# Sixteen heads in six transfers: expanding queries and keys in whole rows instead of halves

## What is computed

```python
y = layernorm(x) * ln_w + ln_b
q, k, v = y @ wq, y @ wk, y @ wv              # per head: 256 x 8, 16 heads
weights = softmax(q @ k.T / sqrt(8) + causal) # 256 x 256 for each batch and head
x1 = layernorm(x + (concat(weights @ v) @ wo + x))
W_all = W + up_aux @ lora_up @ lora_down @ down_aux
out = layernorm(x1 + (x1 @ W_all.T + b))
```

## Time and profile before

| | |
|---|---|
| median of 3 runs | 601.8 us (598.26 to 603.31) |
| the profiled execution | 601.86 us |
| its span, first to last instruction | 599.8 us |
| PE busy | 471.4 us (79%) |
| DVE busy | 356.9 us (60%) |
| ACT busy | 293.9 us (49%) |
| POOL busy | 223.9 us (37%) |
| mean granted clock of PE | 0.836 of 2.4 GHz |
| DMA packets | 91422, of 70.26 MB |

### The profile page before, as it was taken

The page is one execution under the profiler, slowest core; times in us unless marked ns, Lnnn a source line. Parts: engine busy times, 40 slices in busy tenths (PEclk is TensorE's granted clock), DMA queues, the critical chain, the costliest instruction groups (busy, mean ns, idle before and its releaser), DMA issues. The chain is left out here.

```text
span 599.8 us, 26116 instructions
## 1 busy us (share of the span) xinstructions
PE 471.4 (79%) x10929; PEld 381.9 (64%) x10929; DVE 356.9 (60%) x1021; ACT 293.9 (49%) x615; POOL 223.9 (37%) x361
## 2 busy tenths in 40 slices
PE   6897876889888777797766898877785987896793
PEld 3465665677767665676665686666674766774572
DVE  5376555667565656575644765466566656674543
ACT  2625454555455445365543654455544554562470
POOL 6643232442344343243432523334424333422144
PEclk9758888888687799797978977689978878896897
DMA  2544444444444344444434444443444444434210
GB/s 72 153 126 120 125 124 110 115 130 127 126 126 137 112 118 123 130 125 129 136 95 129 126 131 118 127 133 108 129 123 129 126 127 124 128 105 115 74 49 27
DMA packets 91422, 70.26 MB, mean 117 GB/s; under 512 B 14428, under 2 KB 72627, under 8 KB 91315
## 3 DMA queue, kind: packets, MB, share of 16 engines
q1 hardware_dynamic: 89766, 67.69, 39.5%
q10 hardware_dynamic: 1548, 0.95, 0.6%
HBM read 47.07 MB, written 21.00 MB: 113 GB/s over the span
## 5 line engine op out<-in xcount | busy, mean ns | idle before, releaser
L943 DVE TENSOR_REDUCE rowmax<-max_bank 128x2 f32<-128x512 f32 (+3 forms) x352 | 220.4, 639 | 179.8 <-PE max_bank L1249 177.7
L596 ACT ACTIVATE probs<-score_bank 128x512 f32<-128x512 f32 x320 | 182.0, 598 | 139.1 <-PE score_bank L1267 76.0
L1245 PE MATMUL max_bank<-kx,qx 74*64 74x192 bf16 (+2 forms) x1536 | 130.0, 246 | 60.5 <-DMA kx<-k_rows 59.7
L1267 PE MATMUL score_bank<-qx,kx 106*64 106x64 bf16 x2048 | 140.5, 210 | 33.8 <-DMA qx<-mT 33.8
L1245 PEld LDWEIGHTS max_bank<-kx,qx 74*64 74x64 bf16 x1536 | 87.6, 126 | 76.9 <-DMA kx<-k_rows 63.5
L1267 PEld LDWEIGHTS score_bank<-qx,kx 106*64 106x64 bf16 x2048 | 106.9, 123 | 45.8 <-DMA qx<-mT 39.2
L1249 PE MATMUL max_bank<-kx,qx 106*64 106x64 bf16 x2048 | 130.1, 209 | 0.0
L1272 PE MATMUL score_bank<-qx,kx 74*64 74x192 bf16 (+2 forms) x1536 | 122.5, 240 | 0.0
L1289 PE MATMUL pv_bank<-probs,v_ext 128*32 128x256 f32 (+3 forms) x2048 | 97.1, 337 | 13.5 <-issue 13.5
L1249 PEld LDWEIGHTS max_bank<-kx,qx 106*64 106x64 bf16 x2048 | 98.0, 123 | 3.2 <-issue 0.4
L1289 PEld LDWEIGHTS pv_bank<-probs,v_ext 128*32 128x32 f32 x2048 | 63.6, 121 | 46.1 <-issue 29.6
(11 more groups left out here) (99 smaller groups left out, 586.0 us busy)
## 6 DMA issues: line engine op xcount, KB each, us to landing
kx<-k_rows SPq DMA_DIRECT2D x187, 96.0 KB
qx<-q_rows SPq DMA_DIRECT2D x128, 96.0 KB
qx<-q_rows SPq DMA_DIRECT2D x64, 104.0 KB
q_rows<-parts SPq DMA_DIRECT2D x32, 192.0 KB, 2.3
k_rows<-parts SPq DMA_DIRECT2D x31, 192.0 KB, 2.5
xa<-in_x SPq DMA_DIRECT2D x32, 128.0 KB, 2.4
xr<-in_x SPq DMA_DIRECT2D x32, 128.0 KB, 2.3
out<-y SPq DMA_DIRECT2D x32, 128.0 KB, 2.0
```

What stands on the lines that cost most here:

```text
L596: act.activation(probs[:, unit, :], score_bank[SCORE_BANK[unit]][:, :], ACT.Exp, scale=SCALE)\
L943: dve.tensor_reduce(to, b[:, 0:n * width].rearrange("p (w s) -> p w s", s=width), AX.X, ALU.max)\
L1245: pe.matmul(b[which * BLOCK:(which + 1) * BLOCK, at:at + width - BLOCK], q[0:SCORE_ROWS, h, s], k[0:SCORE_ROWS, h, 0:width - BLOCK], start ...
L1267: ins = pe.matmul(b[which * BLOCK:(which + 1) * BLOCK, at:at + BLOCK], k[0:DIAGONAL_ROWS, h, t], q[0:DIAGONAL_ROWS, h, t], start=True, sto ...
```

## The change

`expand` issues six transfers for a batch: three of queries and three of keys, each with all sixteen heads of its 24 (or 26) partitions, so a row is one piece of 8 KB. One semaphore `s_expand` counts them; `max_scores` waits for it at unit 0 alone. The same is done to the transfers of the first batch, two of which ACT issues (five before). In SP's step `load_xa(it, 4)` goes ahead of `store_parts`, and `load_xr` goes behind `expand` and is of the batch `it - 2`. The loads of xa and xr and the expansion have waits and `alone` increments in the loop that stood only in the written-out part. The order of the calls in `first`, `step` and `last` of every engine is a new one, with the same instructions in it; in the loop, PE has two waits fewer (`values`, `x_transpose`) and two more (`pv_transpose` of half 1, `feed_forward`).

```diff
 def load_xa(it, o):
-    if it.static:
-        sp.wait_ge(s_xhat, it.done(o - RING))
-    sp.wait_ge(s_xa, it.done(o - 1, 16))
+    used, landed = it.done(o - RING), it.done(o - 1, 16)
+    sp.wait_ge(s_xhat, used)
+    alone(sp, "sp")
+    sp.wait_ge(s_xa, landed)
...
 def expand(it, o):
...
-    for half in range(HALVES):
-        if half == 0:
-            sp.wait_ge(s_q_stored, it.done(o, 16))
-        else:
-            sp.wait_ge(s_expand[1], it.done(o - 1, EXPAND))
-        for turn in range(PARTS):
-            a, n = turn * PART_ROWS, PART_ROWS + (MAX_PARTS if turn == PARTS - 1 else 0)
-            sp.dma_start(of_half(qx[r][a:a + n, :, :], half), of_half(q[0:n, :, :], half)).then_inc(s_expand[half], 16)
-        if half == 0:
-            sp.wait_ge(s_stored, it.done(o, STORES))
-        for turn in range(PARTS):
-            a = turn * PART_ROWS
-            sp.dma_start(of_half(kx[r][a:a + PART_ROWS, :, :], half),
-                         of_half(k[turn * HD:turn * HD + PART_ROWS, :, :], half)).then_inc(s_expand[half], 16)
+    sp.wait_ge(s_expand, landed)
+    alone(sp, "sp")
+    sp.wait_ge(s_q_stored, q_stored)
+    for turn in range(PARTS):
+        a, n = turn * PART_ROWS, PART_ROWS + (MAX_PARTS if turn == PARTS - 1 else 0)
+        sp.dma_start(qx[r][a:a + n, :, :], q[0:n, :, :]).then_inc(s_expand, 16)
+    sp.wait_ge(s_stored, k_stored)
+    for turn in range(PARTS):
+        a = turn * PART_ROWS
+        sp.dma_start(kx[r][a:a + PART_ROWS, :, :], k[turn * HD:turn * HD + PART_ROWS, :, :]).then_inc(s_expand, 16)
...
 # max_scores
-    if kind == 0 and unit < MAX_UNITS - 1:
-        pe.wait_ge(s_expand[half], it.done(o, EXPAND))
+    if unit == 0:
+        pe.wait_ge(s_expand, it.done(o, EXPAND))
...
 # SP's step
     if it.runs(-7):
         store_y(it, -7)
+    if it.runs(4):
+        load_xa(it, 4)
     if it.runs(1):
         store_parts(it, 1)
     if it.runs(-1):
         load_max_rows(it, -1)
-    if it.runs(-3):
-        load_xr(it, -3)
-    if it.runs(4):
-        load_xa(it, 4)
     if it.runs(1):
         expand(it, 1)
+    if it.runs(-2):
+        load_xr(it, -2)
```

More of the change, by code:

```diff
@@ L736, in first @@
                 exp(at, 1, 5)
+                copy_pv(at, 0, 1)
                 copy_maxT(at, 2)
                 exp(at, 1, 6)
+                copy_v(at, 4)
                 exp(at, 1, 7)
+                exp(at, 1, 8)
                 scale_yT(at, 5)
-                exp(at, 1, 8)
                 exp(at, 1, 9)
@@ L745, in first @@
                 exp(at, 2, 0)
+                exp(at, 2, 1)
+                copy_v(at, 5)
+                exp(at, 2, 2)
+                copy_attnT(at, 0)
+                exp(at, 2, 3)
+                exp(at, 2, 4)
+                copy_maxT(at, 3)
             def step(it):
@@ L766, in step @@
                     scale_yT(it, 4)
+                if it.runs(0):
+                    exp(it, 0, 7)
                 if it.runs(-2):
@@ L777, in step @@
                     exp(it, 1, 0)
+                    exp(it, 1, 1)
+                if it.runs(4):
+                    copy_v(it, 4)
+                if it.runs(1):
+                    exp(it, 1, 2)
+                if it.runs(-1):
+                    copy_attnT(it, -1)
+                if it.runs(1):
+                    exp(it, 1, 3)
+                    exp(it, 1, 4)
+                if it.runs(2):
+                    copy_maxT(it, 2)
             def last(at):
-                copy_attnT(at, 27)
-                exp(at, 29, 1)
-                exp(at, 29, 2)
-                exp(at, 29, 3)
                 copy_pv(at, 28, 1)
-                exp(at, 29, 4)
-                copy_maxT(at, 30)
                 exp(at, 29, 5)
+                copy_zT(at, 27)
                 exp(at, 29, 6)
                 exp(at, 29, 7)
-                copy_zT(at, 27)
+                copy_pv(at, 29, 0)
                 exp(at, 29, 8)
-                copy_pv(at, 29, 0)
                 exp(at, 29, 9)
@@ L1065, in first @@
                 row_max(at, 2, 5)
-                row_max(at, 2, 6)
-                second_rest(at, 4)
             def step(it):
@@ L1071, in step @@
                     scale_ff(it, -4)
+                if it.runs(4):
+                    stats_x(it, 4)
+                if it.runs(0):
+                    row_max(it, 0, 6)
+                if it.runs(2):
+                    second_rest(it, 2)
                 if it.runs(0):
@@ L1103, in step @@
                 if it.runs(1):
+                    row_max(it, 1, 4)
                     row_max(it, 1, 5)
-                    row_max(it, 1, 6)
-                if it.runs(3):
-                    second_rest(it, 3)
             def last(at):
                 scale_ff(at, 25)
+                stats_f(at, 25)
+                row_max(at, 29, 6)
+                second_rest(at, 31)
                 row_max(at, 29, 7)
@@ L1512, in step @@
                     pv(it, -1, 1)
+                if it.runs(0):
+                    scores(it, 0, 0)
+                if it.runs(1):
+                    max_scores(it, 1, 7)
+                if it.runs(0):
+                    scores(it, 0, 1)
                 if it.runs(1):
@@ L1569, in step @@
                     pv(it, 0, 0)
+                    scores(it, 0, 8)
                 if it.runs(2):
```

406 lines of the change are left out of this document (190 added, 216 removed).

## The result

The changed kernel takes 561.9 us (median of 4, 555.8 to 571.0), the kernel before beside it 602.4 us (598.3 to 603.3). The ratio is 0.926, with a 95% interval of 0.918 to 0.935; the executions of the changed kernel fall into faster ones (555.8 and 558.9 us) and slower ones (564.8 and 571.0), the ratio is formed from the faster, and the profiled one is of the slower. Measured again, it took 562.6 us beside 606.8. The direction was forecast, the size was not: 507 us in a range of 478 to 552.

What follows compares the result with a forecast made beforehand. SP's full issue queue was taken as the bound. Span 599.8 us, less 93.5 of PE's DMA waits and 1.2 at the start, plus 2.1 outside the span, gave 507 us, range 478 to 552.

Steps and rivals of the forecast that it cites:

- What bounds the kernel: SP's issue queue is full: its issues set the period of 17.2 us a batch, and PE waits 93.5 us for DMAs.
- Part 1: SP's expansion issues: six 8 KB-row transfers for twelve, 0.80 us each (0.3 to 1.5), SP's cycle from 17.11 to 12.2 us.
- Part 3: Maxima's first unit waits for all six transfers: nothing lost; the chain, 18 us at most, fits the look-ahead of about 20.
- Part 4: New order of calls on PE, DVE, ACT and POOL: same instructions, waits two against two, priced at nothing by itself.
- The sum: Whole kernel: span 599.8 less 93.5 of PE's DMA waits and 1.2 at the start, plus 2.1 outside it: 507 us.
- Part 5: The start: ACT issues two key transfers instead of five and is free 2.9 us earlier; gain 0 to 2.9, taken as 1.2.
- The two terms set against each other: PE's faster clock against its new waits for DVE and ACT: perhaps 1 us a batch each, 30 us in all, cancelling.
- Rival A: Part of the gain returns as PE waits for DVE, ACT or a late expansion: 15.8 us a batch, 555 us; chance 0.16.
- B: PE's clock wins, with fewer stops and more time at 2.4 GHz: 13.0 us a batch, 471 us; chance 0.12.
- C: An issue's price goes by bytes, 1.5 us, so SP stays full at 16.9 us a batch: 593 us; chance 0.04.
- D: Slower: an 8 KB-row issue costs over 1.6 us, perhaps as the queue stands; at 2.0 us, 680 us; chance 0.03.
- E: Issues halve but SP wasn't the bound; the chain with its landings sets the time, within 1% of 602; chance 0.03.

Runs made afterwards that it cites:

- fastest version: The changed kernel with twelve transfers of one 4-KB piece a row instead of six of 8 KB, and its loop written out: 507.1 us, ratio 0.837.

## Why the prediction was wrong

**What bounds the kernel** was right. SP was full: with SP relieved 4 to 11% are won, without that the new order wins nothing (ratio 1.005), and writing out the loop wins 12 us of 606, its 13.5 us of stops being met by 10.9 us more of waits for DMAs.

**Part 1, the price of an issue**, was too high without harm: 0.36 us, near the low end of 0.3 to 1.5 that the earlier trace rows gave, and not the 0.80 taken after the nearest row. What the earlier trace rows share with the new transfer is one piece for a partition; with 2, 4 or 8 KB in it the price is 0.36, with two pieces it was 0.755. The number of pieces alone isn't the rule, though: a store of parts has three pieces of 512 bytes on each of 128 partitions and costs 0.40. What makes the split halves dear is open. SP's slack came out larger than reckoned, and the prediction had said that the price doesn't matter below 1.6 us. It may have mattered the other way: with cheap issues the bytes come in a burst. No run issued the 8 KB rows more slowly.

**Part 3, the chain of the expansion**, had its expansion mis-sized. It had 5.0 us of issuing and 2.5 of landing, 7.5 in all. The issuing is 2.4 us, and from the first issue at 322.54 to the end of PE's wait at 331.71 are 9.2 us, so most of it is the moving of the bytes and not the issuing. The part also said that the maxima's rows stand ahead of the expansion "as before"; it didn't ask for what SP waits there. Once SP has slack, this is a wait of 116 us for the copy of the maxima with the expansion behind it, and putting the expansion ahead moved 25 us of waits for keys away at once. "It fits, without much over" was the sentence that should have had a price: 27 to 35 us of waits for keys are left, and 50 to 55 in the 4 KB versions with the new order. This is the last of the signs that the prediction named for being wrong: waits for keys while SP has slack.

**Part 4, the order**, was priced at nothing. With SP full it is nothing, as the run with twelve transfers showed. With SP relieved the order is worth 16 us, and 23 with pieces of 4 KB (563.7 to 540.7); so the two parts of the change aren't independent, and without this the miss would have been larger.

**The sum** failed at two terms, and here lies the step that made the prediction wrong. It set PE's waits for DMAs from 93.5 to 0; they are 27.2. And it left 13.5 us of stops as they were, with their place named in its first paragraph; they are 58.2. This second is the larger, 44.7 us, and no part of the prediction priced it: Part 1 counted what the new transfers cost the queue that issues them, and not what they cost the others that use the same DMA engines. 507.2 + 27.2 + 44.7 - 14.7 (PE's busy time, which the sum held constant) = 564.4, against 564.8 of the profiled execution. Part of the 44.7 is the order's: with twelve transfers and the new order the stops are 18.9 us, 5.4 more than before; the other 39.3 came with the burst of 8 KB rows. What Part 5 took from the start, 1.2 us, isn't to be seen: all that lies outside of PE's work and these waits fell by 0.4.

**The two terms set against each other** don't cancel. Half of the 30 us of clock came, as 14.7 us less of busy time, though the mean of the granted clock (0.84 against 0.836) hides it; with the stops gone and the loop written out it is 0.94 between 160 and 450 us, and 46.9 us less of busy time than before. The new waits of PE for DVE and ACT, which were to balance it, didn't come: added up over all lines they are 8.8 us where they were 11.7, and even at the fastest version's period of 14.0 us the longest of its waits for a DVE or ACT result is 3.6 us, once.

**Rival A** had nearly the time, 555 us, and a wrong reason for most of it: PE's waits for DVE and ACT didn't grow. Its half sentence on "an expansion that the shorter period makes late again" is right for 27 us. B, C, D and E are excluded by the time; D's queue that stands does occur, in single issues (up to 1957 ns), and not as a rule. (The low end of the forecast, 13.4 us a batch, is 483 us by the prediction's own 507 - 30 x 0.8, not 485; nothing hangs on it.)

**What would show it** named period, SP's waits, PE's waits for keys and the clock, and nothing on stops without a releaser. That splitting the transfers may be faster, which the prediction priced at nothing, was closer than it seemed: halves of 4 KB are 21 us faster. The Trainium skill gives as the reason for splitting DMAs that some may start sooner (Perfetto Trace Analysis, DMA Optimizations). Here it isn't that reason, since unit 0 waits for both halves and its waits for keys grew; the stops became fewer.

That the 4 KB kernel written out takes just the predicted 507 us is luck: 55.4 us of waits for keys that the sum had at zero stand against 46.9 us less of PE busy time and 12.0 us fewer stops, which it had left as they were.

## What to carry to other kernels

When an issuing queue is the bound, ask two things of the cheaper transfer: what it costs the queue (here 0.36 us for one piece on each of 24 partitions against 0.755 for two, whether the piece has 2, 4 or 8 KB), and what a burst at the faster rate does to everybody else on the DMA engines, instruction loads among them. Take the shortest piece that still relieves the queue: here 2 KB in 24 transfers didn't, and 4 KB in twelve beat 8 KB in six by 21 us. And a stall that lies under another bound, as the loop's jumps did, is to be priced anew when that bound goes: 12 us before, 36 after. The mark of a late instruction load is an idle time that nothing ended, at places a fixed number of instructions apart (here 256), just behind a packet of the instruction queue.

## What the runs showed of the hardware

- An issue on SP costs 0.36 us for one piece of 2, 4 or 8 KB on each of 24 partitions, and 0.755 us for two pieces of 2 KB. Bytes and piece size don't show in it. Three pieces of 512 bytes on each of 128 partitions cost 0.40 us, so it isn't the number of pieces alone either.
- Moving the same 67.8 MB, the DMA engines were busy for 50.1% of 563.1 us with the expansion in a burst and for 39.5% of 599.8 us with it spread out, 282 against 237 us. In windows around an expansion it is 181 to 186 GB/s at a busy share of 0.83 to 0.86, and 130 GB/s at 0.46 before: a busy engine moves a quarter less in the burst. It is the rate and not the piece: with 4 KB pieces the busy time is nearly that of 8 KB (50.7% of 537.0 us, 272 us), and the fastest twentieth of the packets of the three sizes take up to 309 ns for 8 KB, 159 for 4 and 81 for 2, nearly the same for a KB, where the medians are 576 and 276 ns in the bursts and 84 when spread out. What the engines meet in a burst, the DRAM side or the 24 partitions that all of them write, was not tried.
- Stops of PE at a jump back were 3 to 4 us each in the kernel before, one at each jump, and up to 7.4 us in the changed one, two at each jump, 5.4 to 8.7 us together.
- PE's instructions come in DMA packets of 16.4 KB, one for 256 instructions. In straight code PE stops for one when the packets are late: 17 times, 26.7 us in the changed kernel written out, 3 times, 1.5 us with pieces of 4 KB, never in the kernel before written out.
